# Chunk stage of a state-space layer: the step sizes move from the inputs into the decays and into B

## The chip, the cores and the metric

One core of a Trainium2 chip runs the whole program. The metric is device time of one execution in microseconds (us); before the change it is 18473.61 us, the median of three executions that lie between 18472.29 and 18473.73.

## The reference, cut to what matters

Two layers run on 8 images of 64 x 64 tokens with 192 channels. Layer 0 holds the part that changes, a state-space recurrence over L = 4096 tokens, in two directions k (row order and column order) with 6 heads each, 64 channels a head, a state of 32:

```python
dt = softplus(dt + dt_bias)          # the step sizes, one per token and head
A = -exp(A_logs)
da = exp(dt * A)
dtx = dt[..., None] * xh             # inputs times steps
h = da_t[..., None, None] * h + dtx_t[..., None] * B_t[:, :, None, :]
y_t = einsum('bhpn,bhn->bhp', h, C_t)
```

Layer 1 has convolutions and a second recurrence ("the scan" below): 192 channels, a state of 16, four directions, 4096 steps, with a decay of its own for every channel and state.

## The kernel before, in words

**Samples and rounds.** The 8 images are samples 0 to 7. Each passes the stages a (projection and depthwise convolution), b (the chunk stage of layer 0), c (gate, output projection, MLP), d, e and f (the front of layer 1, up to the scan's operands), then the scan, then g and h (norm, gate, output). The scan of a sample is cut into 384 units of 128 x 1024 elements. In round r the program runs the 384 scan units of sample r-1, and beside them stages f (its end) of sample r-1, a to f of sample r, and g, h of sample r-2. Round 0 has no scan; round 8 has no a to f of a new sample.

**A scan unit** (`s_slot` of each engine): PE expands the inputs into PSUM (PU, two buffers), DVE multiplies them by B (`PU<-PU,BR`) and runs the recurrence (TENSOR_TENSOR_SCAN into H, line 1762), POOL multiplies by C (HC, line 1929), PE sums over the state (PY), ACT takes the exponentials of the decays (dA) and copies sums and carries.

**The order of work** is written down, not found at run time: every engine runs its list of instructions in order. `Order` lists the steps of the stages; `TAKEN` and `AMID` are tables of digits, one per engine and kind of round (first, middle, last), that say how many of these side steps each engine takes ahead of each part of a scan unit. Semaphores guard the data. The side steps share three PSUM banks in turn (`take_banks`, with `emptied` naming the semaphore that tells when a bank is free).

**Stage b** works on chunks of 128 tokens: 32 chunks by 2 directions, 64 iterations u. `b_setup` computes for all chunks the running sums S1 of dt*A (PE with a triangle of ones), the remaining sums S2, their exponentials ES and exp(S2), and writes S1, transposed and split into three bf16 parts, to DRAM (`spd`). An iteration then is:

- `b_fetch` (SP): two small loads of `spd` into RL in every second iteration, and the chunk's tokens into TK[u % 5], whose columns are C, B and the 384 inputs;
- `b_prepare`: PE transposes C and B and forms S1[t] - S1[s] for 6 heads from RL (rank-3 products); ACT exponentiates them into EE; POOL forms DX (line 1851): inputs times dt, and inputs times dt times exp(S2), 768 columns;
- `b_mix`: PE C·B, ACT copies it to GS, POOL MM = EE times GS (line 1861, 768 columns);
- `b_out` part 0: PE C times carried state (`b_carry`), PE new state = B (128 columns of TK, of which 32 count) against DX's second half in one matmul of 384 columns; POOL fades the old state into HF (line 1874); DVE scales and adds (two operations of 384 columns);
- `b_out` part 1: PE y = MM against DX's first half, six heads of 64 columns; DVE adds it (384 columns);
- `b_store` (SP): y to DRAM.

An f32 matmul stands as two records in the trace (two passes), a transpose or a bf16 matmul as one. "RA" and "RB" are two large SBUF tensors that hold the tiles of all stages; "PB" are the three banks.

Of the kernel before, what the change touches and what calls it, by code (L numbers as in the profile page):

```python
# [9 lines left out]
BF = mybir.dt.bfloat16  # L10
ALU = mybir.AluOpType
ACT = mybir.ActivationFunctionType
# [160 lines left out]
def counts(text):  # L173
    out, n = [], 0
    for c in text:
# [9 lines left out]
        "a000900000000300300200700000200200000200400200000000000000000000000000000000000000000000000000000000g003000000"  # L185
        "00600000060000000600000660000000240000000T00100010900000k00300200800800800500300110700800400900400000260800500"
        "800500000200e0040080060000020090080080070001010080010000060010010000010000000000005000020000005043000000034000"
        "03004003403004702104300700700700700700700700700700700700700700700700700700700700700700700700700700700700700700"
        "70070070070070070070070070070070070070070070070070070070070070070070070070060060100000000000000000800100300000"
        "000600400100000g1000000000090010040060010010030030000020000040030050000040000020020010010030070010030010020010"  # L190
        "02000004003005000001005000002001000103003004003001000002000102003002001000002000003001000003000100000000000000"
        "00000b00100200300400300300200400300500300300400400300300400300300500300300400300300500300300400300300400400300"
        "30040030030050030030040030030030040030030050030040020000000050020000030020010020010030030030020000000000060020"
        "04004001001005003002004002002101001001002003003005008009009009009009009005009009009009009009009000000000000000"
        "00k00000000100300a0020020000020030032000020052000000"),
    ("first", "ACT"): counts(
        "c0000001000009000000204003000000200000007000003005000000300001000003100000001002000000001000000000002000300000"
        "001000500000001001a00000000001b00002002002T00001001000v00000000002m0000000000a10000100100la00000000001n0000000"
        "000a100000001001v0000000000110000100l00a10000100000200000000c0021000000020002000000000041000000000093000000010"
        "02700004003005d00001006003e00000007007e00000007007e00000007007e00000007007e00000007007e00000007007e00000007007"  # L200
        "e00000007007e00000007007e00000007007e00000007007e00000007007e00000007007e0000000600360000000000220000200000000"
        "0005000005400000003000e00000004000b0000600000400000400000100000200a0000040000000005000000000025050000040000000"
        "00005000500002000007002000000004100000002004500000003000300000002002100000002004000002002001000000000000600000"
        "00000120000000100110000100b00a00000000000a00000a001000b00000000000b0000000000b00000000a00100000000b000b0000000"
        "0000b0000000000b00000000b00000000a001000b00001000000c000000020001000020040031000020000015000030030011000000020"
        "0350000100100360000000400250000000000330000100a00800000900i00090000900i000i00009009000900009000000b00000000000"
        "00d0000000014000080010011000040010014000030050010000"),
    ("first", "DVE"): counts(
        "0e090000000070000030000000000080060000000020000000000040030000010000000000000000000000003000000000000000000000"
        "00000000000000O00000000000000000000000000000Q00000000a00000o00000000000a00a00e00000000000a00a00000e00000000a00"  # L210
        "a00000e00000000a00000a00e00000000a00000a00e0000000000060000000000000000090000020010000220000000000000000a00300"
        "40034003043004070034003043043043043043043043043043043043043043043043043043043043043043043043043043043043043043"
        "04304304304304304304304304304304304304304304304304304304304304304304304304303305300002000000000000003301000300"
        "000000601000400001b0050000000090020320050000010040010000030020030200500000040010100200010020320050000100040010"
        "02001002003020050000001005000002001000023020040000031000002000000000000009000002000000000000007000001000002000"
        "00000000000000000000000000000000000000000000000000000000000000000000000000000000000000000000000000000000000000"
        "00000000000000000000000000000000000000000000000000000000000ZZZ200100200200300000300000300300300300000000000500"
        "20050050050000050050000050000000000000000009000000000060089000090090090099000090090090090090090090090030000000"
        "00000000l0700000000300000000000600300700300000000000600"),
    ("first", "POOL"): counts(  # L220
# [183 lines left out]
def emptied(name, i, p):  # L404
# [10 lines left out]
    if name == "b.setup" and p == 4:  # L415
        return [("b_dve", 8), ("b_act", 2)]
# [1997 lines left out]
```

## Time and profile before

| | |
|---|---|
| median of three executions | 18473.61 us |
| the profiled execution's own time | 18471.71 us |
| its span, first to last instruction | 18469.9 us |
| PE busy | 14610.3 us (79%) |
| DVE busy | 14398.6 us (78%) |
| POOL busy | 11453.4 us (62%) |
| ACT busy | 8814.4 us (48%) |
| mean granted TensorE clock | 0.829 |
| POOL line 1861 (MM), 512 times | 925.3 us |
| DVE scans, 3072 times | 5401.9 + 1752.5 us |

The profile's page gives busy time per engine over the whole span and 40 slices of it; these are means over stages that have different limits. Windows of the trace (busy time of each engine in a stretch that one chooses) show each stage for itself, and so do the groups of instructions and the waits inside such a window. PE's busy time is a modelled one, since its matmuls overlap.

### The profile page before, as it was taken

Reading aid. Unit: us, or ns where it says so; the run is one execution under the profiler, and the core shown is the slowest. Engines: PE = TensorE matmul, PEld = TensorE weight load, DVE = VectorE, ACT = ScalarE, POOL = GpSimd, SP = SyncE. Lnnn points to the kernel's source line nnn. Section 1 sums busy time; section 2 is a strip of 40 time slices with the busy share of each in tenths; the row PEclk is TensorE's granted clock in tenths of the full one; section 3 lists DMA queues with packets and bytes.
Section 4 is the critical chain, followed back from the end, with each engine's and each line's share of the span. In section 5 each row is a group of like instructions: output and inputs, shape, how many; then the busy total and the mean of one; then the engine's idle time right before and its main releaser. Section 6 shows DMA issues by size and latency. Waiting matters only on the chain. (4 is left out here: it accounts for less than half of the span.)

```text
span 18469.9 us, 210827 instructions
## 1 busy us (share of the span) xinstructions
PE 14610.3 (79%) x65784; PEld 6340.3 (34%) x65784; DVE 14398.6 (78%) x10538; ACT 8814.4 (48%) x14574; POOL 11453.4 (62%) x5940
## 2 busy tenths in 40 slices
PE   7887789778887788777887778878788778885655
PEld 5433432244332433234332343324433244331202
DVE  2228789777888788877888778887789878889997
ACT  3245345644456444663447534564345644465332
POOL 4226856767557764668547585485755766557563
PEclk9988898798888889788988888879888788876555
DMA  2227567656767577665776657765676756768775
GB/s 87 85 72 208 159 184 178 201 157 182 188 169 206 156 190 190 179 195 153 191 193 191 175 164 190 186 203 161 172 190 176 208 159 184 191 172 217 182 190 141
DMA packets 1553805, 3220.20 MB, mean 174 GB/s; under 512 B 286864, under 2 KB 718800, under 8 KB 1551184
## 3 DMA queue, kind: packets, MB, share of 16 engines
q1 hardware_dynamic: 1552720, 3206.71, 64.8%
q8 instruction: 561, 9.19, 0.2%
q14 instruction: 524, 4.29, 0.1%
HBM read 2474.94 MB, written 731.12 MB: 174 GB/s over the span
## 5 line engine op out<-in xcount | busy, mean ns | idle before, releaser
L1929 POOL TENSOR_TENSOR HC<-H,BR 128x1024 f32<-128x1024 f32 x3072 | 7342.8, 2394 | 4896.6 <-DVE H L1762 2992.6
L1762 DVE TENSOR_TENSOR_SCAN H<-dA,CR,PU 128x1024 f32<-128x1024 f32 x2304 | 5401.9, 2345 | 661.7 <-ACT CR L1179 260.7
L848 PE MATMUL PU<-PT,SELB 96*128 96x512 bf16 x6144 | 2289.0, 461 | 2296.8 <-DVE H L1762 2168.2
L1179 ACT ACTIVATE dA<-dA,A 128x1024 f32<-128x1024 f32 x3072 | 3501.0, 1141 | 1050.1 <-DMA dA<-dld 1003.5
L1546 DVE TENSOR_TENSOR PU<-PU,BR 128x1024 f32<-128x1024 f32 x3072 | 3727.9, 1214 | 314.3 <-PE PU L848 288.0
L848 PE MATMUL PB<-RA,RB 128*128 128x64 f32 (+3 forms) x9120 | 2850.2, 464 | 28.2 <-DVE RA L1549 27.6
L848 PE MATMUL PY<-HC,CB 128*32 128x256 f32 x24576 | 2426.4, 474 | 90.4 <-POOL HC L1929 48.0
L1762 DVE TENSOR_TENSOR_SCAN H<-dA,PU 128x1024 f32<-128x1024 f32 x768 | 1752.5, 2282 | 241.5 <-POOL HC L1929 155.8
L848 PEld LDWEIGHTS PU<-PT,SELB 96*128 96x128 bf16 x6144 | 502.4, 103 | 4158.8 <-issue 3997.5
L848 PEld LDWEIGHTS PB<-RA,RB 128*128 128x128 f32 (+2 forms) x9120 | 1455.5, 196 | 1244.5 <-issue 1176.9
L848 PE MATMUL PB<-RA 128*128 128x384 f32 (+2 forms) x4272 | 1568.0, 502 | 0.0
L1179 ACT ACTIVATE RA<-PB 128x384 f32<-128x384 f32 (+2 forms) x1736 | 793.5, 466 | 1554.5 <-PE PB L848 952.6
L1861 POOL TENSOR_TENSOR RB<-RA,RB 128x768 f32<-128x768 f32 x512 | 925.3, 1807 | 471.5 <-issue 245.3
L848 PE MATMUL PB<-RA,PX 96*128 96x512 f32 x2304 | 1125.5, 627 | 116.2 <-ACT RA L1179 100.2
L1179 ACT ACTIVATE YS<-PY 128x256 f32<-128x256 f32 x768 | 291.7, 380 | 1892.0 <-PE PY L848 1871.0
L848 PEld LDWEIGHTS PY<-HC,CB 128*32 128x32 f32 x24576 | 531.7, 119 | 1719.5 <-issue 1511.7
L848 PEld LDWEIGHTS PB<-RA 128*128 128x128 f32 (+1 forms) x4272 | 823.0, 196 | 762.3 <-issue 507.8
L1179 ACT ACTIVATE RB<-PB 128x128 f32<-128x128 f32 (+4 forms) x1344 | 366.4, 314 | 1297.9 <-PE PB L848 1239.4
L1179 ACT ACTIVATE CR<-H 128x1 f32<-128x1 f32 x3072 | 591.2, 192 | 803.0 <-DVE H L1762 801.3
L848 PE MATMUL PB<-RB 96*128 96x128 bf16 (+2 forms) x6624 | 844.5, 262 | 120.6 <-ACT RA L1179 83.0
L848 PE MATMUL PB<-XT,RB 96*128 96x512 f32 x1536 | 836.3, 685 | 98.4 <-issue 68.6
L848 PEld LDWEIGHTS PB<-RB 128*128 128x128 f32 (+1 forms) x6624 | 725.2, 160 | 193.5 <-ACT RA L1179 88.2
(175 smaller groups left out, 18078.2 us busy)
## 6 DMA issues: line engine op xcount, KB each, us to landing
dA<-dld SPq DMA_DIRECT2D x3072, 512.0 KB, 6.0
PT<-ptd SPq DMA_DIRECT2D x2304, 64.0 KB, 4.3
BR<-bcd SPq DMA_DIRECT2D x256, 512.0 KB, 7.5
ptd<-RA SPq DMA_DIRECT2D x176, 576.0 KB, 5.8
y0d<-RA SPq DMA_DIRECT2D x512, 192.0 KB, 9.6
RA<-y0d SPq DMA_DIRECT2D x128, 768.0 KB, 6.5
yd<-YS SPq DMA_DIRECT2D x768, 128.0 KB, 5.1
tkd<-RB SPq DMA_DIRECT2D x256, 262.0 KB, 4.3
```

The costliest lines, as they stand in the source:

```text
L848: return nc.tensor.matmul(out, w, x, start=start, stop=stop, skip_group_check=True)
L1179: return ac.activation(out, in_, f, **kw)
L1546: return v.tensor_tensor(out, a, b, op)
L1762: v.tensor_tensor_scan(h, a, x, 0.0 if first else K.CR[:, gi:gi + 1], MUL, ADD).then_inc(S["s_scan"], 1)
L1861: po.tensor_tensor(K.MM[u % 2].rearrange("p (h t) -> p h t", h=6), K.EE[u % 2].rearrange("p (h t) -> p h t", h=6), K.GS[u % 2].unsqueeze(1 ...
L1929: po.tensor_tensor(K.HC[:, w % NHC, :], K.H[:, w % NH, :], K.BR[:, (w // 24) % NBR, 1, :], MUL).then_inc(S["s_mulC"], 1)
```

## The change

The product EE·GS·(dt x) can take dt anywhere. After the change ln(dt) is computed once for all chunks (`b_setup`, ACT Ln), S1 - ln(dt) is transposed, split and stored as a second set in `spd`, and RL's weight side is loaded from that set, so that the exponent becomes S1[t] - S1[s] + ln dt[s]: the decays EE carry the step. The y matmuls read the inputs straight from TK. For the state, POOL forms BW = B times dt exp(S2), 6 heads of 32 columns = 192 columns, in place of DX's 768, and PE runs six matmuls of 64 columns (64 columns of BW as weights, 32 of them counting) instead of one of 384. TK is held until y is done: `b_fetch` waits for `b_y` too. Two buffers of 768 columns and one more go, three of 224 come. All tables of `TAKEN` and `AMID` are rewritten.

```diff
 TAKEN = {
     ("first", "PE"): counts(
-        "a000900000000300300200700000200200000200400200000000000000000000000000000000000000000000000000000000g003000000"
+        "a0009000000005300000007200002000008000000000000000000000000000000000000000g03000006000000000006000000600002400"
...
 def emptied(name, i, p):
     if name == "b.setup" and p == 4:
-        return [("b_dve", 8), ("b_act", 2)]
-    if name == "b.setup" and p == 6:
-        return [("b_dve", 13)]
+        return [("b_dve", 8), ("b_act", 3)]
+    if name == "b.setup" and p >= 6:
+        return [("b_dve", 13 if p == 6 else 17)]
...
@@ tensor_steps @@
+        if p == 7:
+            pb = bank(("b.setup", 0, 7))
+            pe.wait_ge(*X.at("b_dve", 10))
+            for j in range(3):
+                t = pe.transpose(pb[:, j * 128:(j + 1) * 128], K.LN[:, j * 128:(j + 1) * 128], K.IDENT)
+            t.then_inc(S["b_pe"], 1)
...
             pe.wait_ge(*X.at("b_dx", u + 1))
-            mm(pst[:, 0:384], tk[:, 32:160], dx[:, 384:768], True, True).then_inc(S["b_carry"], 1)
+            for h in range(6):
+                t = mm(pst[0:64, h * 64:(h + 1) * 64], bw[:, h * 32:h * 32 + 64], tk[:, xo + h * 64:xo + (h + 1) * 64], True, True)
+            t.then_inc(S["b_carry"], 1)
...
             for h in range(6):
-                t = mm(py[:, h * 64:(h + 1) * 64], mx[:, h * 128:(h + 1) * 128], dx[:, h * 64:(h + 1) * 64], True, True)
+                t = mm(py[:, h * 64:(h + 1) * 64], mx[:, h * 128:(h + 1) * 128], tk[:, xo + h * 64:xo + (h + 1) * 64], True, True)
...
@@ scalar_steps @@
+        if p == 3:
+            ac.preload_act_table_set("natural_log_exp_and_others")
+            ac.wait_ge(*X.at("b_dve", 6))
+            ac.wait_ge(*X.at("dt1", 32))
+            act(K.LN, K.DT, ACT.Ln, bias=K.ONE[:, 2:3]).then_inc(S["b_act"], 1)
...
@@ vector_steps, b_setup @@
+            for bw in K.BW:
+                v.memset(bw, 0.0)
...
+            v.wait_ge(*X.at("b_act", 3))
+            tt(S2, p2[:, 0:384], S1, SUB).then_inc(S["b_dve"], 1)
             v.wait_ge(*X.at("b_act", 2))
-            tt(S2, p2[:, 0:384], S1, SUB).then_inc(S["b_dve"], 1)
-            d3 = DT.rearrange("p (u h) -> p u h", u=64)
-            v.tensor_copy(DTT[:, :, 0, :], d3).then_inc(S["b_dve"], 1)
+            tt(K.LN, S1, K.LN, SUB).then_inc(S["b_dve"], 1)
...
+            pb = X.bank(("b.setup", 0, 7))
+            v.wait_ge(*X.at("b_pe", 3))
+            v.tensor_copy(K.SL[:, 0, :], pb[:, 0:384]).then_inc(S["b_dve"], 1)
+            v.wait_ge(*X.at("b_dve", 16))
+            tt(K.S3, pb[:, 0:384], K.SL[:, 0, :], SUB).then_inc(S["b_dve"], 1)
+            v.wait_ge(*X.at("b_dve", 17))
+            v.tensor_copy(K.SL[:, 1, :], K.S3).then_inc(S["b_dve"], 1)
+            v.wait_ge(*X.at("b_dve", 18))
+            tt(K.SL[:, 2, :], K.S3, K.SL[:, 1, :], SUB).then_inc(S["b_dve"], 1)
...
@@ gpsimd_steps, b_prepare @@
         if u >= 3:
-            po.wait_ge(*X.at("b_y", u - 2))
-        po.tensor_tensor(
-            K.DX[u % 3].rearrange("p (w h q) -> p w h q", w=2, h=6),
-            tk[:, xo:xo + 384].rearrange("p (h q) -> p h q", h=6).unsqueeze(1).to_broadcast([128, 2, 6, 64]),
-            K.DTT[:, u, :, :].unsqueeze(3).to_broadcast([128, 2, 6, 64]), MUL).then_inc(S["b_dx"], 1)
+            po.wait_ge(*X.at("b_carry", 2 * (u - 3) + 2))
+        po.tensor_tensor(K.BW[u % 3][:, 0:192].rearrange("p (h n) -> p h n", h=6),
+                         tk[:, 32:64].unsqueeze(1).to_broadcast([128, 6, 32]),
+                         K.DTT[:, u, :].unsqueeze(2).to_broadcast([128, 6, 32]), MUL).then_inc(S["b_dx"], 1)
...
@@ sync_steps, b_fetch @@
-            src = K.spd[:, c * 12:c * 12 + 12, :].rearrange("a h t -> a (h t)")
-            dma(K.RL[c % 2][0:3, 0, :], src, f"rl{c % 2}")
-            dma(K.RL[c % 2][32:35, 1, :], src, f"rl{c % 2}")
+            for w in range(2):
+                dma(K.RL[c % 2][32 * w:32 * w + 3, w, :],
+                    K.spd[w, :, c * 12:c * 12 + 12, :].rearrange("a h t -> a (h t)"), f"rl{c % 2}")
         if u >= 5:
             sp.wait_ge(*X.at("b_carry", 2 * (u - 5) + 2))
             sp.wait_ge(*X.at("b_dx", u - 4))
+            sp.wait_ge(*X.at("b_y", u - 4))
```

What the tables do to the order shows in the instruction lists of the engines. First DVE in stage b of a middle round. The scan is the row with H (before on line 1762, now on 1789), the scan's product with B is `PU<-PU,BR`, and the three rows `RA<-...` with 384 columns are one iteration of stage b. Before:

```order
L1762 SCALAR_TENSOR_TENSOR H<-dA,CR,PU 128x1024
L1546 TENSOR_TENSOR RA<-RA,PB 128x384
L1546 TENSOR_TENSOR PU<-PU,BR 128x1024
L1546 TENSOR_TENSOR RA<-PB,RA 128x384
L1546 TENSOR_TENSOR RA<-RB,PB 32x384
L1762 SCALAR_TENSOR_TENSOR H<-dA,CR,PU 128x1024
```

and now:

```order
L1789 SCALAR_TENSOR_TENSOR H<-dA,CR,PU 128x1024
L1561 TENSOR_TENSOR RA<-PB,RA 128x384
L1561 TENSOR_TENSOR RA<-RB,PB 32x384
L1561 TENSOR_TENSOR PU<-PU,BR 128x1024
L1789 SCALAR_TENSOR_TENSOR H<-dA,CR,PU 128x1024
L1561 TENSOR_TENSOR RA<-RA,PB 128x384
L1561 TENSOR_TENSOR PU<-PU,BR 128x1024
L1789 SCALAR_TENSOR_TENSOR H<-dA,CR,PU 128x1024
```

One iteration of stage b stood beside one scan unit and now stands beside two. On DVE in a middle round the iterations' work spanned scan units 80 to 150 of 384 and now spans 78 to 203; stage c spanned units 152 to 237 and now spans 205 to 252.

The second place is PE in stage c of a middle round. Rows that read `PU<-PT,SELB` and `PY<-HC,CB` are the scan's, the rest is stage c. Before:

```order
L848 MATMUL PU<-PT,SELB 128x512 x2
L848 MATMUL PY<-HC,CB 32x256 x4
L848 MATMUL PB<-XT,RB 128x512 x2
L848 MATMUL PU<-PT,SELB 128x512 x2
L848 MATMUL PY<-HC,CB 32x256 x4
L848 MATMUL PB<-RA,RB 128x512 x2
L848 MATMUL PB<-RA,RB 96x512 x3
L848 MATMUL PU<-PT,SELB 128x512 x2
L848 MATMUL PY<-HC,CB 32x256 x4
```

and now:

```order
L847 MATMUL PU<-PT,SELB 128x512 x2
L847 MATMUL PY<-HC,CB 32x256 x4
L847 MATMUL PB<-XT,RB 128x512 x2
L847 MATMUL PB<-RA,RB 128x512 x2
L847 MATMUL PB<-RA,RB 96x512 x3
L982 MATMUL PB<-CB,RA 128x128 x4
L847 MATMUL PB<-PX,RB 96x512 x6
L847 MATMUL PB<-RA,RB 128x512 x2
L847 MATMUL PB<-XT,RB 128x512 x2
L847 MATMUL PB<-PX,RB 96x512 x6
L847 MATMUL PB<-RA,RB 128x512 x2
L982 MATMUL PB<-CB,RA 128x128 x4
```

Stage c's matmuls stood between all scan units; now about a tile's matmuls stand in one run, of which the excerpt shows the first part (it has 33 matmuls of 512 columns in all), with four scan units between two runs. There are four runs of that length, one shorter ahead of them and one longer behind; before unit 215 and from unit 237 on the matmuls of stage c are spread as they were.

## Rows read from the trace of the kernel before

**Rows 1.** Busy time by window, rounds 4 and 8; x counts instructions.
```profile
core 0: us, PE busy (x) PEld busy (x) DVE busy (x) ACT busy (x) POOL busy (x), PEclk, DMA share, GB/s
...
7878.00:10079.00 2201.00, 1781.31 (x8199) 782.08 (x8198) 1789.48 (x1311) 1097.66 (x1815) 1422.10 (x739) 0.85 0.68 182
...
16708.00:18470.00 1762.00, 1021.81 (x4685) 307.84 (x4683) 1558.69 (x961) 644.03 (x1056) 1020.14 (x433) 0.53 0.71 180
```

**Rows 2.** The same view of round 4: stage b, then stage c.
```profile
8312.00:8830.00 518.00, 386.95 (x2545) 247.32 (x2541) 377.13 (x362) 198.62 (x435) 430.71 (x267) 0.86 0.58 157
8830.00:9286.00 456.00, 401.73 (x1618) 148.09 (x1614) 396.14 (x296) 203.45 (x302) 245.94 (x102) 0.90 0.73 190
```

**Rows 3.** The same windows, and a bare stretch of round 8, scans alone (line 1762).
```profile
8312.00:8830.00 518.00, 178.81 (x77) 0.86 0.58 157
8830.00:9286.00 456.00, 212.29 (x92) 0.90 0.73 190
17400.00:17560.00 160.00, 105.36 (x46) 0.50 0.73 185
```

**Rows 4.** Groups by line and shape, 8354 to 8830: busy us, mean ns, idle before.
```profile
L1929 POOL TENSOR_TENSOR HC<-H,BR 128x1024 f32<-128x1024 f32 x70 | 163.8, 2344 | 0.0
L1861 POOL TENSOR_TENSOR RB<-RA,RB 128x768 f32<-128x768 f32 x63 | 113.9, 1808 | 53.8 <-issue 32.1 <-ACT RB L1179 21.7
...
L1851 POOL TENSOR_TENSOR RA<-RA 128x768 f32<-128x768 f32 x42 | 61.5, 1464 | 1.4 <-DMA RA<-tkd 1.4
...
L1874 POOL TENSOR_TENSOR RB<-RA 32x384 f32<-32x384 f32 x63 | 51.6, 818 | 0.0
...
L1546 DVE TENSOR_TENSOR RA<-PB,RA 128x384 f32<-128x384 f32 x63 | 34.8, 552 | 40.3 <-PE PB L848 40.2
L1546 DVE TENSOR_TENSOR RA<-RB,PB 32x384 f32<-32x384 f32 x63 | 34.1, 542 | 8.0 <-PE PB L848 4.8
...
L1546 DVE TENSOR_TENSOR RA<-RA,PB 128x384 f32<-128x384 f32 x62 | 33.4, 538 | 35.9 <-PE PB L848 35.9
```

**Rows 5.** Waits, 8354 to 8830: us in total, times, longest us.
```profile
DVE RA L1546 <- PE PB L848: 81.0, 69, 6.6
...
PE PB L917 <- DMA RA<-tkd: 68.7, 38, 5.5
...
DVE H L1762 <- POOL HC L1929: 43.8, 35, 1.7
```

**Rows 6.** Busy time by window: stages b and c in round 0, and the bare stretch.
```profile
290.00:596.00 306.00, 243.70 (x1729) 193.39 (x1729) 101.86 (x185) 98.49 (x247) 248.49 (x186) 0.98 0.28 90
622.00:939.00 317.00, 283.07 (x672) 117.31 (x672) 72.17 (x103) 69.80 (x81) 26.08 (x8) 0.93 0.23 71
...
17400.00:17560.00 160.00, 91.06 (x450) 15.25 (x450) 155.91 (x91) 58.75 (x100) 106.10 (x45) 0.50 0.73 185
```

**Rows 7.** PE in time order, round 0: start us, us taken, records.
```profile
398.60 0.81 PE L848 MATMUL PB<-RA 128*128 128x384 f32 x2
399.24 0.81 PE L848 MATMUL PB<-RB,RA 128*128 128x384 f32 x2
```

**Rows 8.** The same view, six y matmuls and what follows them.
```profile
406.90 1.45 PE L848 MATMUL PB<-RA,RB 128*128 128x64 f32 x12
408.18 0.33 PE L848 MATMUL PB<-RB 96*128 96x128 bf16 x3
```

**Rows 9.** DVE in time order, setup of stage b, round 4.
```profile
8336.08 1.70 DVE L1616 COPY RA<-RA 128x384 f32<-128x384 f32 x1
...
8339.30 0.55 DVE L1623 CAST RA<-PB 128x384 bf16<-128x384 f32 x1
8339.88 0.56 DVE L1546 TENSOR_TENSOR RA<-PB,RA 128x384 f32<-128x384 f32 x1
```

**Rows 10.** Groups by line, stage c of round 4 (8944 to 9280).
```profile
L1179 ACT ACT_TABLE_LOAD x14 | 18.0, 1283 | 0.3
```

**Rows 11.** Waits in stage b of round 0 (290 to 596).
```profile
PE PB L917 <- DMA RA<-tkd: 57.5, 52, 1.9
```

More of the change, by code:

```diff
@@ L189 @@
[L189 to L193, printed above, removed]
@@ new lines @@
+    ("middle", "PE"): counts(
+        "0t00000200200400200000200000500400200000600000000000000000000000000000000000g300006000000006000000006000006000"
+        "000600600000T00100100w00100100w00100001w0010010000w00100100w00100100w00100100900000060000200000100000000000500"
+        "02010000042020030070000030040030040030040030040030040034000030040030040030040030040034000030040030040030040030"
+        "04003400003004003004003004003004003004003004003004003004003004003004003004003004003004003004003004003004003004"
+        "00300400300400300400300400300400300400300400300400300400340000300400300400300400300400340000300400300400300400"
+        "300400340000300400300400300400300400300400300400300300300300300100000000000900000300000600400100g10000000000k1"
+        "0000000000k10000000000k10000000000k10000000000j50000200000300300200100010100000300100000300100000000000000000d"
+        "00200400300000300300100100000400g00200400200500b00400300n00400300200200500m00400400300300000700m00300500510050"
+        "000m00500300400200500600f0010010050010060010005000000050010000080010000000000000040040020030030030030030020010"
+        "0000000000b00300340000500100430310300000gd00004009009008009009008702008009009107009005000000000000000000000000"
+        "00k00000e2043032000072020060029050070072000000000000"),
@@ L710, in __init__ @@
         ra, rb = both()
-        self.S0, self.S1, self.S2, self.DT, self.AT, self.ES = (ra(384) for _ in range(6))
-        self.DTT = ra(768).rearrange("p (u w h) -> p u w h", u=64, w=2)
-        self.SB_ = ra(576).bitcast(BF).rearrange("p (a n) -> p a n", a=3)
+        self.S0, self.S1, self.S2, self.DT, self.AT, self.ES, self.LN, self.S3 = (ra(384) for _ in range(8))
+        self.DTT = ra(384).rearrange("p (u h) -> p u h", u=64)
+        self.SB_, self.SL = (ra(576).bitcast(BF).rearrange("p (a n) -> p a n", a=3) for _ in range(2))
         self.HS = ra(768)
@@ L717, in __init__ @@
         self.CC = [ra(256) for _ in range(3)]
-        self.DX = [ra(768) for _ in range(2)] + [rb(768)]
+        self.BW = [ra(224) for _ in range(3)]
         self.EE = [ra(768) for _ in range(2)]
@@ L2012, in b_setup @@
         if p == 7:
-            sp.wait_ge(*X.at("b_dve", 15))
-            for i in range(3):
-                dma(K.spd[i].rearrange("(j q) t -> q j t", q=128), K.SB_[:, i, :].rearrange("p (j t) -> p j t", j=3), "sp")
+            for w, parts_ in enumerate((K.SB_, K.SL)):
+                sp.wait_ge(*X.at("b_dve", (15, 19)[w]))
+                for i in range(3):
+                    dma(K.spd[w, i].rearrange("(j q) t -> q j t", q=128),
+                        parts_[:, i, :].rearrange("p (j t) -> p j t", j=3), "sp")
     def b_fetch(u, p):
```

281 lines of the change are left out of this document (137 added, 144 removed).

## The prediction

> **What bounds the kernel now.** The place of the time is found in three steps. First the windows by round: each of the rounds 2 to 7 takes about 2200 us, and in such a round neither DVE (1789 of 2201 us busy) nor PE (1781) is full [rows 1], so the loss lies in single stages. Then the windows of one middle round by stage. Stage b takes 518 us, with POOL busy for 431 and DVE for 377; stage c takes 456 us, with PE busy for 402 and DVE for 396 [rows 2]. The reader should see that a different engine leads in each. Last the scans in the same windows: 77 in stage b, 92 in stage c [rows 3], so a scan unit costs 518/77 = 6.7 us beside stage b and 456/92 = 5.0 us beside c. In a bare stretch 45 units fit into 160 us [rows 6], 3.56 us each, and DVE is the full engine there (155.9 us busy).
>
> Why 6.7? One iteration of b goes with one unit, and POOL then runs 2.34 + 1.81 + 1.46 + 0.82 = 6.43 us of work a unit [rows 4]. POOL is the pace. DVE waits for PE (81 us) and for POOL (44 us), and PE waits 69 us for token loads [rows 5].
>
> **The POOL term.** 192 columns replace 768. The trace has no such instruction. The nearest rows are 384 columns in 0.82 us and 768 columns in 1.46 us [rows 4]; a straight line through them gives 0.50 us for 192, which I take. The bounds are 0.82 (the smaller neighbour, no gain below 384 columns) and a quarter of 1.46, 0.37. That frees 0.96 us of POOL an iteration (0.64 to 1.09), 61 us a sample. At the old order this alone would make POOL's work 5.47 us a unit.
>
> **The PE term.** The state matmul was two records of 384 columns, 0.64 us apart [rows 7]; now it is twelve of 64 columns. The twelve y records of 64 columns with 128 columns of weights take 1.28 us from first start to the next instruction [rows 8]. So the new state costs 0.64 us (no change) to 1.28 us (+0.64 an iteration), and I take the middle, +0.3. The weights are only 64 columns here. The Trainium skill (TensorE: Matmul & The Clock Gate, section LDWEIGHTS) says that a weight load's time goes with its columns, not its rows; by that rule each record needs half the load of a y record and the term would be about 0. Nothing in the total hangs on it, since PE does not lead in b: a scan unit needs 91.06/45 = 2.02 us of PE at half clock, 1.01 at full, an iteration of b 243.7 us over 61 iterations, 4.0 us [rows 6], so beside half an iteration PE has 3.0 to 3.3 us a unit.
>
> **The order.** It decides the result, since one iteration now stands beside two units. I go through a middle round, by scan units.
>
> Stage b, units 72 to 204, 132 of them. DVE has 3.56 us plus half of 0.552 + 0.542 + 0.538 [rows 4], 0.82: 4.37 us. POOL has 2.34 + (1.81 + 0.82 + 0.50)/2 = 3.91. DVE becomes the leader with POOL at 89% behind it; with BW at its upper bound POOL has 4.07, still below. 132 x 4.37 = 577 us. Some waits must stay, so I add 4%: 600 us. Bounds: 577, and 4.8 us a unit = 634 (close to the 5.0 us that a unit costs beside stage c today). The added wait, SP's for y of iteration u-5, stands right behind the store of that y, which waits for later work, so it costs nothing; behind it are the decay loads of the scan, and those would be late if it did. The token loads had two iterations (13 us) to land, now nearly 18, so PE's 69 us of waiting should mostly go.
>
> Stage c, units 204 to 252, 48 of them. Alone, in round 0, stage c takes 317 us with PE busy for 283 [rows 6], so it is limited by PE and its chains. 48 units add 1.01 us of PE each: 365 us, and 5 us for the hand-over, 370. Bounds: the scan fills PE's idle 34 us, 336; or every run of matmuls and every group of four units come one after the other, 410 (first rival).
>
> Together 970 us for 180 units, where 974 us (518 + 456) went for 168. The other stages keep their work and have 12 units fewer beside them. A unit less saves 3.56 us where DVE leads, 1.0 to 2.0 us where PE does: 12 to 43 us, I take 28. Middle round: 970 - 974 - 28 = -32 us. I give round 1, whose b and c are the same work, the same. Seven rounds: -224 us.
>
> Setup of b, once a sample: DVE loses a copy of 1.70 us and gets one subtraction, four operations of 384 columns at about 0.5 [rows 9] and three memsets, +2 us; ACT gets Ln and a table load of 1.28 us [rows 10]; PE three transposes. The new operations form a chain with hops between engines, and the scan stands behind it on DVE. I take +4 us a sample (0 to 10), +32 us in all.
>
> Round 0 has no scan. An iteration takes 306/61 = 5.0 us there with POOL busy for 81% [rows 6], and PE waits for token loads [rows 11]; the load of iteration u+5 is queued behind the store of y on SP, and that loop stays. I take 0; if POOL were the pace it would give 61 us. Round 8 has no stage b: 0.
>
> Sum: 18471.7 (the profiled execution's own time; the median is 18473.6, 2 us above, which I neglect) - 224 + 32 = **18,280 us**, 1.0% faster. About 0.2%, 37 us, can be told from no change.
>
> **Rivals.**
>
> *The runs of stage c (slower).* PE gets 33 matmuls of 512 columns in a row, then four scan units. PU has two buffers, so DVE can be only two units ahead; during a run it stops after two units, and in the four units after it PE waits for scans. Per group of four that is up to (4 - 2) x 3.56 = 7.1 us of PE idle. Twelve groups' worth over 48 units is 85 us, on 317 us: 402, with 8 us for the hand-overs 410. That is +40 a round against my 370, so +8 a round, 56 + 32 = +88: 18,560. It decides from 397 us on, where b's gain is used up, and is a clear loss above 402. For it: the in-order lists, and in stage c today the pieces of matmul are short and PE is 88% busy all the same. Against it: the longer stretches at the stage's two ends are not in runs, and PE was full in most of c already.
>
> *Both stages at their bounds (faster still).* 577 + 336 = 913, -89 a round with the 28: -623 + 32 gives 17,880. For it: DVE is 97% busy in the bare stretch [rows 6] with the same three-engine loop. Against: no stretch with side work comes to that.
>
> *Waits stay in stage b (no change).* DVE's 81 us of waiting for PE [rows 5] are a matter of three shared banks, not of POOL. If a unit costs 4.75 us, stage b takes 627 us, the round changes by -5, the whole by -35 + 32 = -3: 18,470. For it: those waits stand in stage b of every round. Against: the engines in front of the banks get 9 us for an iteration where they had 6.7.
>
> *TensorE's clock (much slower).* In stage b the granted clock is 0.86 with PE busy for 75% [rows 2]; in the bare stretch it is 0.50, the lower of the two levels all the time, with 57% [rows 6]. Spread out, b loads PE for 3.0 to 3.3 of 4.55 us at full clock, 66 to 73%. At the lower level PE would need 2 x 3.0 = 6.0 us a unit, 792 us for b, +160 a round: 19,600. The Trainium skill (the same page, section Terms) has a block that watches how busy PE is and gates its clock, which is this mechanism; whether the load here is dense enough no row shows.
>
> **How the numbers follow.** My case, with its own range 18,100 to 18,430: 0.48. Faster still: 0.14. No change: 0.13. The runs of stage c: 0.22. The clock: 0.03. So faster 0.62, same 0.13, slower 0.25. The range: down to 17,900, where the second rival ends; up to 18,620, a little over the first one. About 0.1 lies below and 0.1 above.
>
> **What would show it.** In the changed trace: BW near 0.50 us; stage b of round 4 near 4.55 us a unit, DVE busy for over 90% and POOL for under 90%, granted clock above 0.8; PE's waits for token loads under 20 us; stage c near 370 us with PE over 95% busy. I am wrong if stage c takes 400 us or more with DVE idle in blocks, if b stays above 4.8 us a unit, or if setup costs more than 10 us a sample.

## The result, and the profile after

The changed kernel takes 18783.2 us (median of four executions, 18776.6 to 18795.7), the kernel before, run beside it on the same chip, 18473.7 us. The ratio is 1.0169, with a 95% interval of 1.0157 to 1.0181: **1.7% slower, +310 us**, where 18,280 us was forecast and the range ended at 18,620. The profiled execution has a span of 18774.4 us.

The place is found with windows over the stages of a round. The four windows of round 4 below are, in order: the end of f with a, then b, then c, then d to f. They are cut where PE takes the first step of the next stage. First the kernel before:

```profile
core 0: us, PE busy (x) PEld busy (x) DVE busy (x) ACT busy (x) POOL busy (x), PEclk, DMA share, GB/s
7882.00:8333.00 451.00, 346.26 (x1517) 148.40 (x1514) 338.70 (x226) 258.40 (x439) 277.87 (x154) 0.84 0.68 188
8333.00:8856.00 523.00, 393.50 (x2604) 250.67 (x2603) 382.94 (x363) 200.42 (x439) 443.85 (x274) 0.86 0.58 162
8856.00:9289.00 433.00, 391.68 (x1536) 143.73 (x1536) 376.15 (x280) 197.57 (x291) 229.77 (x95) 0.91 0.74 190
9289.00:10093.00 804.00, 659.12 (x2571) 242.84 (x2570) 701.79 (x448) 451.27 (x661) 479.44 (x222) 0.83 0.72 188
```

The same four stages of the changed kernel:

```profile
8026.00:8472.00 446.00, 343.87 (x1501) 148.57 (x1499) 337.54 (x225) 263.55 (x445) 272.97 (x153) 0.84 0.66 188
8472.00:9138.00 666.00, 512.03 (x3797) 292.33 (x3796) 568.07 (x476) 263.93 (x561) 510.56 (x329) 0.85 0.67 182
9138.00:9512.00 374.00, 340.42 (x1155) 133.06 (x1156) 238.87 (x205) 150.45 (x206) 139.33 (x57) 0.92 0.59 154
9512.00:10282.00 770.00, 640.07 (x2416) 241.65 (x2414) 649.23 (x418) 427.34 (x621) 444.96 (x207) 0.82 0.70 183
```

Scans counted between the same steps give the units. The means over rounds 2 to 7:

| stage | before: us, units | changed: us, units | difference |
|---|---|---|---|
| end of f, and a | 449.4, 74 | 446.1, 72 | -3 |
| b | 523.2, 81 | 662.6, 136 | +139 |
| c | 432.2, 86 | 372.6, 48 | -60 |
| d to f | 804.2, 143 | 769.3, 128 | -35 |
| round | 2209.0 | 2250.6 | +42 |

Round 1 has +52 us, round 0 up to the first scan +6, round 8 -3. Together 6 x 41.6 + 52 + 6 - 3 = 305 us, all of the difference between the two profiled executions (304.5); the medians differ by 310.

So stage b took 55 more units and paid 2.5 us for each; the others gave up 55 and saved 98 us, 1.8 us each. In b a unit costs 662.6/136 = 4.9 us, above the 4.8 at which the prediction called itself wrong. Stage c is as forecast (372.6; 370 was said). The waits of b (units 81 to 153) that answer to [rows 5]: us in total, times, longest.

```profile
ACT dA L1187 <- DMA dA<-dld: 95.0, 44, 5.8
...
PEld PB L847 <- ACT RA L1187: 62.4, 43, 5.0
...
DVE RA L1561 <- PE PB L847: 42.3, 30, 5.0
```

PE no longer waits for token loads. In their place ACT waits 95 of 349 us for the decay tiles of the scan, and since its list is in order, b's copies stand behind that wait; PE waits for those copies, DVE for PE. The small prices came out as written. Groups by shape in that window:

```profile
L1877 POOL TENSOR_TENSOR RA<-RA 128x192 f32<-128x192 f32 x36 | 18.2, 506 | 0.0
...
L847 PE MATMUL PB<-RA 128*64 128x64 f32 x432 | 41.7, 262 | 0.2 <-DVE RA L1561 0.2
```

BW takes 0.506 us (0.50 was forecast), and the 12 state records of an iteration together 41.7/36 = 1.16 us of modelled, overlapping time at a granted clock of 0.88.

### The profile page after: what moved, and what is told of

It reads as the page before. It is cut to its first block and busy times, and to the rows that moved or that the text cites. A ratio compares the mean times of both kernels' runs of the same rounds, so it can differ in the third digit from the quotient of the medians.

```text
span 18774.4 us, 221235 instructions
## 1 busy us (share of the span) xinstructions
PE 14885.4 (79%) x70928; PEld 6535.2 (35%) x70928; DVE 14372.8 (77%) x10595; ACT 8794.4 (47%) x14591; POOL 10958.6 (58%) x5940
## 5 line engine op out<-in xcount | busy, mean ns | idle before, releaser
L847 PE MATMUL PB<-RA,RB 128*128 128x64 f32 (+3 forms) x11136 | 3021.0, 421 | 140.3 <-ACT RB L1187 116.6
L847 PEld LDWEIGHTS PB<-RA,RB 128*128 128x128 f32 (+2 forms) x11136 | 1674.3, 191 | 1337.3 <-issue 1159.9
L847 PE MATMUL PB<-RA 128*64 128x64 f32 (+3 forms) x9728 | 2045.3, 361 | 10.0 <-DVE RA L1561 5.7
L847 PEld LDWEIGHTS PB<-RA 128*64 128x64 f32 (+2 forms) x9728 | 1095.2, 175 | 1059.1 <-issue 845.5
L847 PE MATMUL PB<-RB 96*128 96x128 bf16 (+1 forms) x4608 | 601.5, 251 | 593.0 <-ACT RA L1187 572.4
L1187 ACT ACTIVATE RA<-PB 128x384 f32<-128x384 f32 (+2 forms) x1736 | 747.6, 456 | 500.9 <-PE PB L847 393.2
```

Of the source, the lines that this page charges most:

```text
L847: return nc.tensor.matmul(out, w, x, start=start, stop=stop, skip_group_check=True)
L1187: return ac.activation(out, in_, f, **kw)
```

## The experiments

Four theories stood at some point. **Order**: the rewritten tables cost the time. **Arithmetic**: the new product, matmuls and setup do. **Queue**: SP's queue of DMAs paces stage b. **Engines**: POOL or DVE does. All kernels were timed beside the kernel before.

**old_order.** The tables of before for rounds 2 to 7, on all five engines and in AMID, with the steps of b's setup two units behind their new places; nothing else.

```diff
 TAKEN = {
     ("middle", "PE"): counts(
-        "0t00000200200400200000200000500400200000600000000000000000000000000000000000g300006000000006000000006000006000"
+        "0t000000004003003000002000003004002000004004000000000000000000000000000000000000000j000000060000060000060024"
...
```

> Edit: the changed arithmetic, with the tables of the kernel before for the middle rounds (rounds 2 to 7; only the steps of b's setup, which have a longer chain now, keep their new places, two units later). Rounds 1 and 8 keep the new tables. Theory A (the new order is the loss: b at 4.92 us a unit instead of 4.55, 48 units in c, the end of the round packed): the middle rounds come back to 2203 us or less, and since POOL works 0.96 us less an iteration, stage b takes 460 to 518 us; whole time 18,300 to 18,510 us. Theory B (the new arithmetic costs: twelve short state matmuls on PE, a longer setup, a longer hold of the token tiles): the middle rounds stay at 2240 us or more, whole time 18,700 to 18,850 us.

18565.6 us, ratio 1.0054 (1.0037 to 1.0070). Rounds 2 to 7 take 2210.8 us on average (2209.0 before), stage b 529.5. Round 1, which keeps the new tables, stays at 2113. So the order caused the loss: the arithmetic changes a middle round by 2 us. But the half of theory A that concerned POOL fell. Stage b did not come down to 460 to 518, although POOL had 0.96 us less an iteration. Its window (b of round 4), and the largest waits in its units 81 to 153:

```profile
8382.00:8911.00 529.00, 422.47 (x3247) 274.12 (x3246) 383.62 (x366) 203.37 (x443) 383.14 (x274) 0.85 0.56 161
```

```profile
DVE RA L1561 <- PE PB L847: 116.0, 129, 7.4
...
POOL RB L1886 <- ACT RB L1187: 92.8, 25, 7.5
...
PEld PB L922 <- DMA RA<-tkd: 63.2, 36, 6.2
```

POOL went from 444 to 383 us of work, and the time that was freed turned into a wait of 92.8 us for GS (16.9 us in the kernel before, units 81 to 153). PE still waits for tokens. POOL had not been the pace of b at all.

**new_order.** The kernel before, its arithmetic as it was, with all the new tables of TAKEN and AMID.

```diff
     ("middle", "PE"): counts(
-        "0t000000004003003000002000003004002000004004000000000000000000000000000000000000000j00000006000006000006002400"
+        "0t00000200200400200000200000500400200000600000000000000000000000000000000000g300006000000006000000006000006000"
...
```

> Edit: the arithmetic of the kernel before (DX of 768 columns) with the new tables in all rounds. POOL then has 0.96 us more an iteration, 3.91 + 0.48 = 4.39 us a unit in stage b, as much as DVE's 4.37. Theory A (order is the loss, and POOL does not pace b in the new order): 18,780 to 18,950 us, b at 4.9 to 5.2 us a unit. Theory B (the arithmetic costs): under 18,700 us. A third reading (in the new order POOL's work counts in full): b at 4.92 + 0.48 = 5.40 us a unit, 63 us a round, 19,200 us.

18739.4 us, ratio 1.0143 (1.0128 to 1.0158), just under the interval given for theory A. Stage b takes 653.9 us, a round 2244.3. Adding 0.96 us of POOL an iteration cost nothing, as taking it away had gained nothing. The new arithmetic is 6 us a round dearer in this order (2250.6), with stage b 9 us longer; that is where the twelve short state matmuls stand, but they were not tried alone.

**small_rl.** The loads of the running sums bring 128 of 1536 columns from the third chunk on.

```diff
-                dma(K.RL[c % 2][32 * w:32 * w + 3, w, :],
-                    K.spd[w, :, c * 12:c * 12 + 12, :].rearrange("a h t -> a (h t)"), f"rl{c % 2}")
+                n = 12 if c < 2 else 1
+                dma(K.RL[c % 2][32 * w:32 * w + 3, w, 0:n * 128],
+                    K.spd[w, :, c * 12:c * 12 + n, :].rearrange("a h t -> a (h t)"), f"rl{c % 2}")
```

> Edit: the changed kernel, but from the third chunk on the two loads of the running sums in b_fetch bring 128 of their 1536 columns; the decays of those chunks are computed from old sums, so that the values of this part are left out. It asks whether the sync engine's time for these two loads (1.6 to 3.9 us each for 9 KB) is what makes the decay tiles of the scan late, on which ACT waits 126 us in stage b with b's copies behind it in its list. Theory S (that queue paces b): b falls from 4.92 to 4.6 us a unit or below, 18,450 to 18,600 us in all. Rival (the late tiles are covered, or come late for another reason): 18,740 to 18,790 us, no change.

18739.5 us, ratio 1.0141 (1.0126 to 1.0156); b's units 72 to 204 take 641 us (647), and the whole is 44 us or 0.2% shorter than the changed kernel: an effect, but a small one, and theory S falls. What it taught is in SP's own records: an issue of this load takes 2.72 us on average with 0.77 KB as with 9 KB (2.73). So the time of the issue does not go with the size of the load; it looked like a wait for what stands ahead, and in both16 below it is 0.34 us. SP in the changed kernel, in time order (start, us taken):

```profile
8559.25 5.27 SPq L1995 DMA_DIRECT2D RB<-spd  x2
8564.63 0.34 SPq L1995 DMA_DIRECT2D RA<-tkd  x1
8565.02 2.03 SPq L1995 DMA_DIRECT2D dA<-dld  x2
8567.10 0.59 SPq L1995 DMA_DIRECT2D yd<-YS  x1
8568.11 0.33 SPq L1995 DMA_DIRECT2D y0d<-RA  x1
8568.54 0.53 SPq L1995 DMA_DIRECT2D RA<-tkd  x1
8570.36 2.79 SPq L1995 DMA_DIRECT2D dA<-dld  x1
8573.25 1.50 SPq L1995 DMA_DIRECT2D PT<-ptd  x3
8574.79 0.52 SPq L1995 DMA_DIRECT2D dA<-dld  x1
```

The token load that starts at 8568.54 is one of an odd iteration, in column order.

**tk7_old.** old_order with seven token tiles, each load two iterations earlier.

```diff
-        self.TK = [ra(524) for _ in range(5)]
+        self.TK = [ra(524) for _ in range(6)] + [rb(524)]
...
-        if u >= 5:
-            sp.wait_ge(*X.at("b_carry", 2 * (u - 5) + 2))
...
+        for v in range(3) if u == 0 else [u + 2] if u + 2 < 64 else []:
+            if v >= 7:
+                sp.wait_ge(*X.at("b_carry", 2 * (v - 7) + 2))
...
```

> Edit: as old_order (changed arithmetic, the tables of before in the middle rounds), with seven token tiles instead of five, and each token load issued two iterations earlier. In old_order PE waits about 60 us for token loads in 477 us of stage b (units 81 to 153), although nothing in POOL is full any more. Theory T (the loop fetch, five tiles, store is what paces b in the old order at 6.6 us a unit): b's units 72 to 204 fall from 821 us to 720 or less in each middle round, whole time 17,900 to 18,300 us. Rival D (the sync engine's queue or the transfers themselves are full, so that an earlier place in the queue gives nothing): 810 to 825 us, whole time within 30 us of old_order, 18,540 to 18,600 us.

18587.8 us, ratio 1.0054 (1.0039 to 1.0069), as rival D said; stage b 531 us. The waits for tokens went, and these came in their place:

```profile
PEld PB L847 <- DMA RB<-spd: 56.1, 21, 7.6
PE PB L847 <- DMA RB<-spd: 50.0, 17, 7.3
```

The wait only moved to the next load in the same queue. That spoke against a load that is issued too late, and for a queue whose transfers take too long.

**act_fetch and act_fetch_old.** b_fetch issued by ACT, at its place in ACT's list, in the new and the old order.

```diff
@@ scalar_steps @@
+    def dma(out, in_, name):
+        return ac.dma_start(out, in_).then_inc(S[name], 16)
+    def b_fetch(u, p):
+        ...
+        ac.wait_ge(*X.at("b_carry", 2 * (u - 5) + 2))
...
```

> Edit: the changed kernel with its own tables, b_fetch issued by ACT instead of SP. ACT waits 95 us of 349 for the scan's decay tiles there. Theory Q (SP's queue makes them late): units 72 to 204 fall from 647 us to 610 or less, whole time 18,500 us or less. Rival D (transfers as such, or PE and DVE with the three banks, set 4.9 us a unit): 635 to 650 us, whole time 18,700 to 18,790. Rival A (ACT held up by its issues): slower, 18,830 or more.

> Edit: as old_order, with b_fetch (running sums and tokens) issued by ACT instead of SP, at its place in ACT's list. In stage b SP spends 399 of 477 us inside issues, 162 us of them in the loads of running sums of 2.8 us each. Theory Q (that one queue, in which every transfer stands behind the ones before it, paces b): units 72 to 204 fall from 821 us to 760 or less, whole time 18,200 us or less. Rival D (all transfers together are the limit, or another engine): 805 to 825 us, whole time 18,500 to 18,600. Rival A (ACT's list is held up by the issues, 0.5 us or more each, with scan decays behind them): slower, 18,650 or more.

19154 us (1.0362, 1.0346 to 1.0377) and 19310 us (1.0432, 1.0407 to 1.0457): much slower, as rival A had it, but not in the way it said. In the new order 209 us of what it loses against the changed kernel (371 us by the medians) lie in round 0, where there is no scan and no decay to hold up. PE waits there for token loads, 94 of 306 us and up to 6.2 us at a time; in the changed kernel the same wait is 51.8 us and never over 1.5 (us in total, times, longest):

```profile
PEld PB L922 <- DMA RA<-tkd: 93.7, 18, 6.2
```

b's units 72 to 204 take 665 us in the middle rounds (647). SP's issues are short now (0.53 us for a decay load), and still the decay loads of units 81 to 153 land late (count, KB each, median us from issue to landing; 11.0 us in the changed kernel):

```profile
dA<-dld SPq DMA_DIRECT2D x72, 512.0 KB, 9.4
```

So the blocked issues on SP were a symptom. Behind both queues something else was late.

**light_tk.** Token loads bring 70 columns from the sixth iteration on; the inputs of those iterations are left out.

```diff
-            dma(K.TK[u % 5], K.tkd[c * 128:(c + 1) * 128, :], f"tki{u % 5}")
+            n = 524 if u < 5 else 70
+            dma(K.TK[u % 5][:, 0:n], K.tkd[c * 128:(c + 1) * 128, 0:n], f"tki{u % 5}")
...
-            dma(K.TK[u % 5][:, 0:454], tkc[c][:, :, 70:524], f"tki{u % 5}")
+            n = 454 if u < 5 else 70
+            dma(K.TK[u % 5][:, 0:n], tkc[c][:, :, 70:70 + n], f"tki{u % 5}")
```

> Edit: the changed kernel with its own tables; from the sixth iteration on the token load brings 70 of 524 (454) columns, so that the inputs of those iterations are old ones; this part of the computation is left out. It takes 0.2 MB off each iteration, about a sixth of the bytes in stage b, and leaves the number of issues as it is. Theory V (the bytes on the DMA engines, 184 GB/s in this stretch, set b's pace): units 72 to 204 fall from 647 us to 600 or less, whole time 18,450 us or less. Rival Q (the queue's issues or the order, not the bytes): 635 to 650 us, whole time 18,700 to 18,790.

18219.3 us, ratio 0.9855 (0.984 to 0.987). b's units 72 to 204 take 569 us, 4.2 us a unit from unit 81 on (4.84 in the changed kernel), decay tiles land after 5.3 us. Theory V's numbers came true, but its reason was doubtful: the DMA engines had been busy for only two thirds of the time. The packet records settle what to look at. Counts of packets that start in each microsecond from 8576 on, changed kernel; 1816 bytes is the column-order token load, 4096 the decays:

```
us from 8576   0   1   2   3   4   5   6   7   8   9  10  11
1816 bytes     7  16  14  12  20  22  13  11   0   0   0   0
4096 bytes    11  45  51   6   0   2   6   5  11   3  49  45
busy engines  18  16  18   5   2   2   2   2   3  10  19  14
```

("Busy engines" is the sum of the packets' times in that microsecond; packets overlap a little, so that it can pass 16.) From 8580 to 8584 two engines carry the rest of one token load while a decay load that was issued at 8574.79 has packets left on those two. The windows view has the same: first a stretch with a full queue, then this one.

```profile
8566.00:8569.00 3.00, 1.49 (x8) 0.76 (x8) 3.00 (x4) 2.36 (x5) 3.00 (x2) 1.00 0.99 293
8580.00:8584.00 4.00, 4.00 (x24) 1.89 (x23) 3.32 (x3) 0.00 (x0) 1.71 (x1) 0.56 0.14 50
```

A share of 0.14 is 2.2 engines of 16. The load's access pattern in DRAM is `c w h n` with w = 2 outermost. The Trainium skill (DMA: Bandwidth & Descriptors, section Why a DMA increments its semaphore by 16 and not by 1) says that a transfer is spread over the largest number of engines, up to 16, that divides the slowest dimension of both its patterns; here that is 2, and the trace agrees.

Round 0 of act_fetch shows what that does to a load behind it. A column-order load goes out there from 402.96 to 410.08 us. The row-order load that is issued at 403.88 has 112 of its 128 packets out by 406.42, which is the share of fourteen engines, and the last 16, the share of two, only from 410.32 to 410.98. PE waits for that load and starts at 410.59. So two engines were behind in that run too. Why its loads come so close to their use when ACT issues them was not followed.

**both16 and load16.** Column-order load and store as two DMAs of 64 partitions, so that the outermost dimension is 64 on both sides; in load16 the load alone. Same bytes, more issues.

```diff
-            dma(K.TK[u % 5][:, 0:454], tkc[c][:, :, 70:524], f"tki{u % 5}")
+            for w in range(2):
+                dma(K.TK[u % 5][64 * w:64 * w + 64, 0:454], tkc[c][w][:, 70:524], f"tki{u % 5}")
...
-        dma(ycol[c] if k else K.y0d[0, c * 128:(c + 1) * 128, :], K.YO[u % 4], f"yo{u % 4}")
+        yo = K.YO[u % 4]
+        if k == 0:
+            dma(K.y0d[0, c * 128:(c + 1) * 128, :], yo, f"yo{u % 4}")
+        else:
+            for w in range(2):
+                dma(ycol[c][w], yo[64 * w:64 * w + 64], f"yo{u % 4}")
```

> Edit: the changed kernel with its own tables; in odd iterations of b (column order) the token load and the store of y are issued as two DMAs of 64 partitions each, whose outermost dimension is 64 on both sides, instead of one with an outermost dimension of 2. In the trace the 128 packets of a column load of 1816 bytes go out over 7 us, for several us of which exactly two of the 16 DMA engines are busy; everything later in the queue waits for those two. Theory E (that uneven load paces b, in either order of the steps): the packets of a column load go out within 3 us, decay tiles land after 5 to 6 us instead of 9 to 10, b's units 72 to 204 fall from 647 us to 520 to 560, as with the light loads, round 0 falls by 20 us or more; whole time 18,100 to 18,350 us. Rival V (the bytes in all): 630 to 650 us, whole time 18,700 to 18,790. Rival I (the additional issues on SP cost more than they give): 18,800 or more.

> Edit: as both16, but only the token load is split; the column store of y stays one DMA with an outermost dimension of 2. The store moves 192 KB in 128 packets that go out over about 5 us. Theory E with both transfers at fault: between the changed kernel and both16, 18,250 to 18,550 us, b's units 72 to 204 at 560 to 600 us. Rival (the load alone matters, since the store has no one waiting for it): within 40 us of both16.

both16: 18112.6 us, ratio 0.9803 (0.9788 to 0.9817). load16: 18174.1 us, 0.9836 (0.9821 to 0.9851). Theory E holds in each of its numbers: b's units 72 to 204 take 558 us, the first scan starts at 1359.7 us instead of 1401.1, the 128 packets of a column load go out within 1.9 us (mean of 18) where they had taken 7.9 (mean of 17). All bytes are still moved, so V falls. The load is 609 of the 671 us: load16 ended between the two figures for it, 62 us above both16 where the rival said 40 at most, and 76 us under the 18,250 of theory E with both at fault. I had given the store too much. The DMA view of units 81 to 153, the changed kernel first, then both16 (count, KB each, median us from issue to landing):

```profile
dA<-dld SPq DMA_DIRECT2D x72, 512.0 KB, 11.0
y0d<-RA SPq DMA_DIRECT2D x36, 192.0 KB, 10.0
```

```profile
dA<-dld SPq DMA_DIRECT2D x72, 512.0 KB, 5.1
RA<-tkd SPq DMA_DIRECT2D x18, 262.0 KB, 3.2
RA<-tkd SPq DMA_DIRECT2D x36, 113.5 KB, 4.0
y0d<-RA SPq DMA_DIRECT2D x37, 96.0 KB, 3.9
```

And stage b of both16 in round 4, 572 us where the changed kernel had 666; DVE is busy for 98% of it. From unit 81 on a unit costs 4.20 us, the same as with the light loads, so in both runs DVE is the limit of b:

```profile
8157.00:8729.00 572.00, 451.09 (x3797) 259.82 (x3796) 561.60 (x477) 263.39 (x561) 511.09 (x329) 0.97 0.79 212
```

**both16_old and both16_before.** The same split in old_order, and in the kernel before.

```diff
@@ old_order, and the kernel before, b_fetch and b_store alike @@
+            for w in range(2):
+                dma(K.TK[u % 5][64 * w:64 * w + 64, 0:454], tkc[c][w][:, 70:524], f"tki{u % 5}")
...
+            for w in range(2):
+                dma(ycol[c][w], yo[64 * w:64 * w + 64], f"yo{u % 4}")
```

> Edit: as both16, with the tables of the kernel before in the middle rounds (old_order with the two split transfers). Theory E: in the old order b is then bound by its engines, POOL at 5.47 us and DVE at 5.2 us a unit with a whole iteration beside it: units 72 to 204 fall from 821 us to 730 to 770, a middle round from 2211 to about 2140; whole time 18,000 to 18,250 us, so about the same as both16 or faster. If the new order is the better one once the queue is free, both16 wins by 50 us or more. Rival V: 18,540 to 18,600 us, as old_order.

> Edit: the kernel before, with its arithmetic and tables, and the two transfers split in the same way. POOL has 6.43 us of work a unit in stage b then, and this time it should be the pace: Theory E: units 72 to 204 at 790 to 815 us (821 before, round 1 as well), whole time 18,350 to 18,470 us, 100 us or more above both16_old: only here does the smaller product on POOL pay. Rival (POOL is never the pace): equal to both16_old within 60 us.

both16_old: 17764.4 us, ratio 0.9615 (0.960 to 0.9629). both16_before: 17983.1 us, 0.973 (0.9714 to 0.9746). Both are faster than I wrote. I had put POOL at one iteration a unit; b has 64 iterations for 81 units, its setup included. "As fast as both16 or faster" came out at 348 us faster. Stage b of round 4, first both16_before, then both16_old:

```profile
8118.00:8576.00 458.00, 358.87 (x2604) 227.79 (x2603) 377.02 (x362) 204.06 (x440) 443.00 (x274) 0.95 0.69 186
```

```profile
8038.00:8456.00 418.00, 376.41 (x3246) 246.71 (x3242) 377.50 (x366) 202.12 (x443) 382.65 (x274) 0.95 0.75 204
```

With the queue free, POOL is busy for 443 of 458 us: now it is the pace, and now the smaller product pays, 40 us in stage b of every middle round. The two kernels are 219 us apart; both16_old still has the new tables in rounds 1 and 8, which the next one takes away.

**best.** both16_old with the old tables in rounds 1 and 8 too: the new arithmetic, the old order, the split transfers.

```diff
     ("first", "PE"): counts(
-        "a0009000000005300000007200002000008000000000000000000000000000000000000000g030000060000000000060000006000024"
+        "a000900000000300300200700000200200000200400200000000000000000000000000000000000000000000000000000000g0030000"
...
```

> Edit: both16_old, with the tables of the kernel before in round 1 as well (there too only the steps of b's setup keep the places of the new tables, moved with the stage); so: the changed arithmetic, the order of before in all rounds, the two split transfers. In round 1 the old order took 2065 us and the new one 2113 to 2126 before the queue was free, and both16_before took 2002 us in round 1 with the larger products. Order theory: round 1 falls from 2026 us in both16_old to 1955 to 1975, whole time 17,690 to 17,730 us, ratio to before 0.957 to 0.960. Rival (the order no longer matters in round 1): 2015 to 2030 us, whole time 17,750 to 17,780.

17682.2 us, ratio 0.9574 (0.9561 to 0.9587). Round 1 takes 1956 us, as the theory said (the whole is 8 us below its figure). It is 4.3% faster than the kernel before and 5.9% faster than the changed one. Against both16_before, which has the same order throughout, the new arithmetic is worth 301 us (about 290 by the ratios, since the two were timed on different chips): a gain that the queue had covered. And against both16, which differs in the order alone, the old order is worth 430 us (about 420 by the ratios).

The middle rounds side by side, us in each stage (units as in the first table for old and new order):

| | order | end of f, a | b | c | d to f | round |
|---|---|---|---|---|---|---|
| before | old | 449 | 523 | 432 | 804 | 2209 |
| changed | new | 446 | 663 | 373 | 769 | 2251 |
| both16_before | old | 450 | 459 | 431 | 804 | 2144 |
| both16 | new | 448 | 572 | 373 | 767 | 2160 |
| best | old | 449 | 418 | 428 | 806 | 2101 |

## Why the prediction was wrong, step by step

**"POOL is the pace" of stage b: wrong, and this carried the rest.** This is the step that failed. The row behind it [rows 2] has POOL busy for 431 of 518 us, 83%; I reached 6.43 of 6.7 us a unit by counting a whole iteration per unit. [rows 4] has 63 iterations beside 70 units in 476 us, 0.9 of an iteration a unit, and so 2.34 + 0.9 x (1.81 + 1.46 + 0.82) = 6.0 us of POOL in 6.8 us, 88% and not 96%; with the setup, stage b has 81 units for its 64 iterations. That left room for something else, and old_order and new_order show that 0.96 us of POOL an iteration is worth nothing in either order.

**What did set the pace** was two DMA engines. From the packet records: in round 0 a column load keeps them for 4.9 us (64 packets each of 0.076 us), the column store for 4.2 (64 of 0.066), and their sixteenth of the row-order load and store for 1.6, so 10.7 us for two iterations; round 0 takes 2 x 5.0 = 10.0 [rows 6]. A scan unit brings each engine 2.4 us of decays and operands (these packets fill 50% of all engines' time in 349 us with 72 units). Stage b with 81 units then needs 32 x 10.7 + 81 x 2.4 = 537 us (523 measured), with 136 units 669 us (663 measured). That is an estimate, and its closeness is partly luck: it takes the packet times of round 0, and with the longer ones of stage b itself (0.09 to 0.10 us for a column load's packet, which overlap) the same sum gives about 565 and 730 us. What shows the cause is both16, which takes only the unevenness away. It explains what stood in [rows 6] from the start: an iteration of 5.0 us in round 0 with POOL at 81% and no engine full.

**The b term: 4.55 us a unit was 4.90, 647 us where 600 were forecast.** In my sum, 55 more units beside b cost 82 us (600 - 518), 1.5 each, since I took b's 6.7 us a unit for POOL's and thought that it would go with the product. They cost 139, 2.5 each, the two engines' 2.4. I had read the token waits as latency that more time per iteration would heal. They did vanish, but the lateness moved to the decay loads in the same queue. The rival "waits stay in stage b" was the nearest one; I put the waits to the banks, and priced them at 4.75. DVE, which I had at over 90% in b, is busy for 568 of 666 us, 85%. With the queue free my model of b does hold: both16 needs 558 us for the 132 units, a little under the 577 that DVE's work gave.

**The c term: right** (units 204 to 252: 370 forecast, 374 measured; PE is busy for 340 of 374 us, 91%, not over 95%), and with it the first rival was wrong: no loss from runs of matmuls, though DVE is idle in blocks (239 of 374 us busy) as that rival said.

**The term for the other stages: right, against a baseline that was cut too early.** Forecast -28, measured -24 (the units outside 72 to 252, against those outside b and c before). But my 974 us for b and c before began with DVE's first setup step, at 8312 [rows 2]; from PE's first step on, at 8333, the two take 955 us, and I let the new 970 replace 19 us too many. So the forecast of -32 a round missed the measured +42 by 74: 47 in b, 4 in c, 19 in the baseline, 4 here.

**Setup and round 0: inside their bounds.** +6 us up to the first scan against +4 a sample with a bound of 10; old_order's middle rounds are +2 with everything of the new arithmetic in them. The state matmuls were taken as +0.3 us an iteration. At full clock the carry, the state and the two transposes behind them took 1.67 us in the kernel before (398.60 in [rows 7] to the end of the first row here) and take 2.07 us now:

```profile
399.89 0.38 PE L848 MATMUL PB<-RA 128*128 128x128 f32 x2
```

```profile
407.05 2.07 PE L847 MATMUL PB<-RA 128*128 128x384 f32 x16
```

So the term is about +0.4 us. The Trainium skill's rule on a weight load's columns (TensorE: Matmul & The Clock Gate, section LDWEIGHTS), by which it would be about 0, shows inside the group: a record with 64 columns of weights starts 0.058 us after the one before it, a y record with 128 columns 0.106. But the group as a whole came out at my middle or a little over it, not at 0. It cost little, since PE does not lead: with everything else of the new arithmetic 6 us a round in the new order.

**The clock: right.** In b it is granted 0.85, with 0.86 before. With the queue freed it is 0.97 (both16), with PE busy for 79% of the stage where it had been 77%. The clock rose together with the freed queue and was not tried by itself; where DVE is busy for 98% it is not what sets the time.

**That the new order is the better one: wrong with or without the queue's trouble.** The gain forecast for it rested on the 6.7 us that a unit cost beside b. With the queue free the new order is still the slower one, 2160 against 2101 us a round: 55 units moved to b cost 154 us there, where DVE is then full, and save 95 elsewhere. Why c and d to f give back so little per unit was not tried. So the change as it stood would miss its forecast with the queue free too: both16 is 130 us slower than both16_before. The order brings the loss in either case; what the queue took away was the gain of the arithmetic.

## What to carry to other kernels

When no engine is full in a stage, look at the DMA queue before believing in the busiest engine: issues on SP that take microseconds, transfers that land in 10 us where they elsewhere land in 5, and waits that move from one load to the next when a load is issued earlier. Then look at short windows for a low DMA share, here 0.14, about two engines of 16: a transfer with an outermost dimension of 2 held up the loads behind it. And a product that is made smaller gained only where its engine was the pace; here the same edit was worth nothing with the queue full and about 300 us with it free. Count the work of an engine per unit over the whole stage, and hold it against the engine's busy share there: 6.43 of 6.7 us did not agree with 83%.

## What the runs showed of the hardware that was not expected

- A column-order load of 227 KB in 128 packets took 7.9 us on two engines in stage b of the changed kernel; as two loads of 64 partitions, 1.9 us. A packet of it takes 0.10 us there.
- SP's time in an issue is no property of the transfer: the 9 KB load took 2.73 us on average behind the slow transfers in the changed kernel, 0.34 us in both16.
- A second issuing queue (act_fetch) shortened SP's issues from 1.15 to 0.53 us for a decay load, but it landed after 9.4 us all the same (11.0 before, 5.1 in both16): a queue of its own did not help a load that two engines held up.
